# Two graph layers on one core: bit-packed adjacency stored per pair of groups, and catching up from tile 12 instead of 16

## What is computed

```python
def layer0(x, adj, weight, bias):
    a = adj.astype(x.dtype)
    x1 = a @ x / jnp.sum(a, axis=1, keepdims=True)
    return jnp.concatenate([x1, x], axis=1) @ weight + bias

def layer1(x, adj, W, a):
    h = jnp.einsum('ni,oi->no', x, W)
    e = (h @ a[:128])[:, None] + (h @ a[128:])[None, :]
    e = jnp.where(adj == 0, -jnp.inf, e)
    return jax.nn.softmax(e, axis=1) @ h

x = layernorm(x + layer0(x, adj, ...))
x = layernorm(x + layer1(x, adj, ...))
```

## Time and profile before

| | us |
|---|---|
| median of 3 runs | 1045.35 |
| lowest, highest | 1044.92, 1046.54 |
| the profiled execution, its own time | 1044.53 |
| its span, first to last instruction | 1042.8 |
| TensorE (PE) busy | 998.2 (96%) |
| VectorE (DVE) busy | 686.2 (66%) |
| ScalarE (ACT) busy | 607.9 (58%) |
| GpSimd (POOL) busy | 288.5 (28%) |

### The profile page before, as it was taken

How to read it: one execution, slowest core, us unless ns; L and a number is a source line. 1 busy time by engine, 2 the same in 40 slices (tenths; PEclk the granted TensorE clock), 3 DMA queues, 4 the chain that set the end, 5 groups by cost and what they waited for, 6 DMA issues and landing times.

```text
span 1042.8 us, 22097 instructions
## 1 busy us (share of the span) xinstructions
PE 998.2 (96%) x8783; PEld 872.1 (84%) x8783; DVE 686.2 (66%) x1647; ACT 607.9 (58%) x618; POOL 288.5 (28%) x275
## 2 busy tenths in 40 slices
PE   7898988999999999999999999999999999999996
PEld 6787867878888888888888888888888888888885
DVE  2677677787777767777676665555545765566564
ACT  2897798888888888888767676767421000000000
POOL 4344444443544445344332232222000000000000
PEclk8999999999999999999999999999999999999999
DMA  9999999999999999999999999999321112222101
GB/s 273 354 417 424 421 421 420 421 421 421 421 422 420 421 416 419 417 419 419 400 385 366 356 346 349 330 337 312 144 82 73 50 45 85 87 87 87 29 27 33
DMA packets 52569, 306.94 MB, mean 294 GB/s; under 512 B 6768, under 2 KB 8432, under 8 KB 19312
## 3 DMA queue, kind: packets, MB, share of 16 engines
q0 software_dynamic: 37344, 270.03, 65.5%
q1 hardware_dynamic: 14288, 34.71, 9.7%
q10 hardware_dynamic: 832, 0.75, 0.3%
HBM read 287.08 MB, written 18.38 MB: 293 GB/s over the span
## 4 chain that ended last, share of the span: by engine, by line
PE 63%; DMA 25%; ACT 6%; issue 3%; DVE 1%; POOL 1%; ACTq 0%; DVEq 0%
PE ps_agg L373 34%; DMA adj_in<-in_adj_dram,chunk 24%; PE ps_part L373 23%; ACT edges L562 5%; PE ps_y L373 4%; DMA x_all<-in_x_dram 1%; POOL adj_in L1335 1%; PE ps_h L745 1%; PE ps_h L683 1%; ACT parts L554 0%; PE ps_x1T L738 0%; ACT L578 0%; DVE partial L890 0%; DVE edgesT L921 0%; PE ps_y L683 0%
## 5 line engine op out<-in xcount | busy, mean ns | idle before, releaser
L373 PE MATMUL ps_agg<-parts,edgesT 128*128 128x257 f16 (+1 forms) x5248 | 606.2, 275 | 26.2 <-DVE edgesT L921 26.0
L373 PEld LDWEIGHTS ps_agg<-parts,edgesT 128*128 128x128 fp8e4 x5248 | 513.6, 98 | 106.0 <-DVE edgesT L921 30.5
L562 ACT ACTIVATE edges<-adj_in 128x2048 fp8e4<-128x2048 int32 x256 | 480.7, 1904 | 68.9 <-DMA adj_in<-in_adj_dram,chunk 68.6
L1335 POOL DMA_INDIRECT adj_in<-in_adj_dram,chunk x256 | 283.5, 1107 | 442.0 <-ACT edges L562 429.9
L921 DVE STREAM_TRANSPOSE edgesT<-edges 128x512 uint32<-128x512 uint32 x256 | 168.4, 691 | 71.5 <-ACT edges L562 70.7
L373 PE MATMUL ps_part<-parts,edgesT 128*128 128x258 f16 x1664 | 194.7, 273 | 0.0
L373 PEld LDWEIGHTS ps_part<-parts,edgesT 128*128 128x128 fp8e4 x1664 | 162.7, 98 | 22.8
L628 ACT ACTIVATE std<-mean_var,eps 128x1 f32<-128x1 f32 x64 | 18.9, 295 | 234.2 <-DVE mean_var L1158 234.2
L934 DVE SCALAR_TENSOR_TENSOR packed<-edgesT,packed 128x2048 uint32<-128x2048 uint32 x48 | 109.8, 2287 | 0.0
L373 PE MATMUL ps_part<-parts,packed 128*128 128x258 f16 x784 | 90.6, 273 | 0.0
L373 PEld LDWEIGHTS ps_part<-parts,packed 128*128 128x128 fp8e4 x784 | 76.6, 98 | 11.1
(11 more groups left out here) (118 smaller groups left out, 658.8 us busy)
## 6 DMA issues: line engine op xcount, KB each, us to landing
adj_in<-partial_sums SPq DMA_DIRECT2D x16, 258.0 KB, 5.8
adj_in<-in_adj_dram,chunk POOLq DMA_INDIRECT x256, 12.7
out_dram<-edges SPq DMA_DIRECT2D x60, 64.0 KB, 3.1
partial_sums<-partial SPq DMA_DIRECT2D x13, 258.0 KB, 7.2
packed_adj<-packed SPq DMA_DIRECT2D x3, 1024.0 KB, 9.5
adj_in<-packed_adj SPq DMA_DIRECT2D x2, 896.0 KB, 7.3
adj_in<-packed_adj SPq DMA_DIRECT2D x2, 832.0 KB, 4.9
x_all<-in_x_dram POOLq DMA_DIRECT2D x6, 256.0 KB, 10.0
```

The costliest lines, as they stand in the source:

```text
L373: done = eng.matmul(bank[:, 0:cols], rows[:, n // BYTES, n % BYTES, :], moving[:, n, :], start=(n == first), stop=(n == last))
L562: act.activation(edges[:, r // 2, r % 2, :], adj_in[:, m % SLOTS, :], ACT.Copy, scale=EDGE[t % GROUP], saturate=False).then_inc(s_conv, 1)
L1335: pool.indirect_dma_start(adj_in[:, m % SLOTS, :], None, adj_chunks, bass.IndirectOffsetOnAxis(chunk[:, 0:1], 0), element_offset=first_row ...
```

## The change

Two groups 2p and 2p + 1 (for the first 14 groups, `PAIRS` = 7) are joined into one word array: the odd group's words are shifted up by one bit and or-ed with the even group's (`join`), in place in `packed[:, 1]`, and stored once. The bits kept are now 4, 6, 2 and 0, so that the bit above each is free, and the edge values are 128, 128, 192 and 144. Groups 14 and 15 are stored alone. The second pass loads each group's words from its pair's store and takes the tile's bit out with one shift and mask. On VectorE the join of a pair stands in step 8p + 8 in the place of `pack`, whose two calls follow in step 8p + 9; the checks of the odd groups come in steps 8p + 7 and 8p + 8. On SyncE the partial sums are now stored ahead of the words. Catching up runs in tiles 12 to 23 with 2, 3 and 3 bands, in the bank `ps_small`, from two loads instead of three.

```diff
--- before.py
+++ after.py
@@ -48,8 +48,8 @@
     EARLY = FIRST_INLINE * GROUP
-    CATCH = 16
-    CAUGHT = [3, 3, 2]
+    CATCH = 12
+    CAUGHT = [2, 3, 3]
     CTILES = GROUP * len(CAUGHT)
     CWORDS = P * max(CAUGHT)
@@ -73,11 +73,14 @@
-    EDGE = [128.0, 128.0, 128.0, 192.0]
-    KEPT = [0x10, 0x20, 0x40, 0x04]
-    FOREIGN = 0x8B
-    UNPACKED = [2.0 ** -5, 2.0 ** -3, 2.0, 2.0 ** -6]
-    BIT_SCALE = [bit / edge for bit, edge in zip(UNPACKED, EDGE)]
+
+    EDGE = [128.0, 128.0, 192.0, 144.0]
+    KEPT_BIT = [4, 6, 2, 0]
+    KEPT = [1 << bit for bit in KEPT_BIT]
+    FOREIGN = 0x8A
+    UNPACKED_BIT, UNPACKED = 4, 2.0 ** -5
+    BIT_SCALE = [UNPACKED / edge for edge in EDGE]
+    PAIRS = GROUPS // 2 - 1
     def every_byte(b):
         return b * 0x01010101
@@ -99,7 +102,15 @@
     def last_turn(j):
         return turn_of[GROUP * loads[j] + GROUP - 1]
-    packed_dram = nc.dram_tensor("packed_adj", (GROUPS, P, TW), u32, kind="Internal").ap()
+
+    def store_of(g):
+        return g // 2 if g < 2 * PAIRS else g - PAIRS
+
+    def stored_bit(g, c):
+        return KEPT_BIT[c] + (g % 2 if g < 2 * PAIRS else 0)
+
+    STORES = store_of(GROUPS - 1) + 1
+    packed_dram = nc.dram_tensor("packed_adj", (STORES, P, TW), u32, kind="Internal").ap()
     part_dram = nc.dram_tensor("partial_sums", (GROUPS, P, GROUP * HCOLS), fp32, kind="Internal").ap()
     h_dram = nc.dram_tensor("g_h_rows", (N, HCOLS), fp32, kind="Internal").ap()
     x1_dram = nc.dram_tensor("g_x1_rows", (N, F), fp32, kind="Internal").ap()
@@ -181,9 +192,10 @@
         CBLOCK = 36
         late = parts1[:, CBLOCK:NBLK, :].rearrange("p n f -> p (n f)").bitcast(u32)
-        sizes = [len(CAUGHT) * CWORDS, 2 * CWORDS, len(CAUGHT) * GROUP * HCOLS, HCOLS]
+        c_loads = store_of(len(CAUGHT) - 1) + 1
+        sizes = [c_loads * CWORDS, 2 * CWORDS, len(CAUGHT) * GROUP * HCOLS, HCOLS]
         ends = list(itertools.accumulate(sizes))
-        c_in = late[:, 0:ends[0]].rearrange("p (k w) -> p k w", k=len(CAUGHT))
+        c_in = late[:, 0:ends[0]].rearrange("p (k w) -> p k w", k=c_loads)
         c_words = late[:, ends[0]:ends[1]].rearrange("p (k w) -> p k w", k=2)
         c_part = late[:, ends[1]:ends[2]].bitcast(fp32).rearrange("p (k c f) -> p k c f", k=len(CAUGHT), c=GROUP)
         c_lo = late[:, ends[2]:ends[3]].bitcast(fp32)
@@ -206,7 +218,7 @@
         ps_h = ps("ps_h")
         ps_small = ps("ps_small")
         sums = [ps_agg[0], ps_agg[1], ps_part, ps_y]
-        ps_caught = ps_catT
+        ps_caught = ps_small
@@ -239,6 +251,7 @@
         s_tr = sem("quarter_transposed")
         s_check = sem("checked")
         s_pack = sem("tile_packed")
+        s_joined = sem("pair_joined")
         s_pkst = sem("packed_stored")
         s_agg = sem("agg_summed")
@@ -287,7 +300,7 @@
         s_vord = sem("verdict_steps")
         s_flag = sem("flag_made")
-        s_cld = [sem(f"caught_words_landed{k}") for k in range(len(CAUGHT))]
+        s_cld = [sem(f"caught_words_landed{k}") for k in range(c_loads)]
         s_cunp = sem("caught_words_unpacked")
         s_csum = sem("caught_summed")
         s_clo = sem("caught_lo_copied")
@@ -424,11 +437,15 @@
             sp.dma_start(w1_sb[:, :], w1).then_inc(s_const1, 16)
             sp.dma_start(a2_sb[:, :], a1[F:2 * F].rearrange("(p o) -> p o", o=1)).then_inc(s_const1, 16)
-            def store_group(g):
-                words = slice(bands_of(g) * P, TW)
-                sp.wait_ge(s_pack, GROUP * (g + 1))
-                wait(sp, s_pkst, 16 * g)
-                sp.dma_start(packed_dram[g][:, words], packed[:, g % 2, words]).then_inc(s_pkst, 16)
+            def store_words(g):
+                n, words = store_of(g), slice(bands_of(g - 1 if g < 2 * PAIRS else g) * P, TW)
+                if g < 2 * PAIRS:
+                    sp.wait_ge(s_joined, n + 1)
+                else:
+                    sp.wait_ge(s_pack, GROUP * (g + 1))
+                    sp.wait_ge(s_check, CHECKS * g)
+                wait(sp, s_pkst, 16 * n)
+                sp.dma_start(packed_dram[n][:, words], packed[:, g % 2, words]).then_inc(s_pkst, 16)
             def store_partial(g):
                 sp.wait_ge(s_partk, GROUP * (g + 1) - EARLY)
@@ -437,35 +454,34 @@
             def load_caught(k):
                 sp.wait_ge(s_pkst, 16 * (k + 1))
-                sp.dma_start(c_in[:, k, 0:P * CAUGHT[k]], packed_dram[k][:, 0:P * CAUGHT[k]]).then_inc(s_cld[k], 16)
+                sp.dma_start(c_in[:, k, :], packed_dram[k][:, 0:CWORDS]).then_inc(s_cld[k], 16)
             def store_caught(k):
                 sp.wait_ge(s_ckept, GROUP * (k + 1))
                 sp.dma_start(part_dram[k], c_part[:, k, :, :].rearrange("p c f -> p (c f)")).then_inc(s_cst, 16)
             for g in range(GROUPS - 1):
-                store_group(g)
                 if g >= FIRST_INLINE:
                     store_partial(g)
-                if g == 2:
-                    load_caught(0)
-                    load_caught(1)
-                if g == 3:
-                    load_caught(2)
+                if g % 2 == 1 or g >= 2 * PAIRS:
+                    store_words(g)
+                if g % 2 == 1 and store_of(g) < c_loads:
+                    load_caught(store_of(g))
                 if 0 <= g - CATCH // GROUP < len(CAUGHT):
                     store_caught(g - CATCH // GROUP)
-            sp.wait_ge(s_pkst, 16 * (GROUPS - 1))
+            sp.wait_ge(s_pkst, 16 * (STORES - 1))
             sp.wait_ge(s_check, CHECKS * (GROUPS - 1))
             words0 = slice(done_of(0) * P, TW)
-            sp.dma_start(packed[:, 0, words0], packed_dram[0][:, words0]).then_inc(s_pkld[4], 16)
-            store_group(GROUPS - 1)
+            sp.dma_start(packed[:, 0, words0], packed_dram[store_of(0)][:, words0])\
+                .then_inc(s_pkld[4], 16)
+            store_words(GROUPS - 1)
             store_partial(GROUPS - 1)
             def load_group(j):
                 g, s = loads[j], (j - 1) % 4
                 words = slice(done_of(g) * P, TW)
-                sp.wait_ge(s_pkst, 16 * (g + 1))
-                sp.dma_start(packed_in[:, s, words], packed_dram[g][:, words]).then_inc(s_pkld[s], 16)
+                sp.wait_ge(s_pkst, 16 * (store_of(g) + 1))
+                sp.dma_start(packed_in[:, s, words], packed_dram[store_of(g)][:, words]).then_inc(s_pkld[s], 16)
                 if g >= FIRST_INLINE:
                     sp.wait_ge(s_partst, 16 * (g - FIRST_INLINE + 1))
                 sp.dma_start(part_in[:, s, :], part_dram[g]).then_inc(s_partld[s], 16)
@@ -754,7 +770,7 @@
             def caught(i):
                 blocks = GROUP * CAUGHT[i // GROUP]
                 if i == 0:
-                    pe.wait_ge(s_xTlc, GROUPS - AHEAD)
+                    pe.wait_ge(s_shift, 1)
                 pe.wait_ge(s_cunp, i + 1)
                 wait(pe, s_ckept, i)
                 contract(pe, ps_caught, c_words[:, i % 2, :], parts1, range(blocks), 0, blocks - 1).then_inc(s_csum, 1)
@@ -925,8 +941,10 @@
                 dve.wait_ge(s_tr, NQ * (t + 1))
                 bits, word = edgesT[:, t % 2, :], packed[:, g % 2, :]
                 if c == 0:
-                    wait(dve, s_pkst, 16 * (g - 1))
-                    wait(dve, s_check, CHECKS * (g - 1))
+                    if g % 2 == 0:
+                        wait(dve, s_joined, g // 2)
+                    else:
+                        wait(dve, s_pkst, 16 * (g // 2))
                     dve.tensor_single_scalar(word, bits, every_byte(KEPT[c] | FOREIGN), ALU.bitwise_and)\
                         .then_inc(s_pack, 1)
                 else:
@@ -941,6 +959,13 @@
                 dve.scalar_tensor_tensor(stray[:, :], packed[:, g % 2, part * width:(part + 1) * width],
                                          every_byte(FOREIGN), stray[:, :],
                                          ALU.bitwise_and, ALU.bitwise_or).then_inc(s_check, 1)
+
+            def join(p):
+                words = slice(bands_of(2 * p) * P, TW)
+                dve.wait_ge(s_pack, 2 * GROUP * (p + 1))
+                dve.wait_ge(s_check, 2 * CHECKS * (p + 1))
+                dve.scalar_tensor_tensor(packed[:, 1, words], packed[:, 1, words], 1, packed[:, 0, words],
+                                         ALU.logical_shift_left, ALU.bitwise_or).then_inc(s_joined, 1)
             def degree(t):
                 dve.wait_ge(s_agg, t + 1)
@@ -1028,6 +1053,8 @@
                 blk = slice(QBLK * s, QBLK * (s + 1))
                 dve.tensor_reduce(x_big[:, blk], parts0[:, blk, 0:F], AX.X, ALU.max, apply_absolute_value=True)\
                     .then_inc(s_xbig, 1)
+
+            odd_groups = range(1, 2 * PAIRS, 2)
             def step(t):
                 if on(t, 0) and t > 0:
@@ -1051,16 +1078,24 @@
                     moments_joined(t - 1)
                 if inline(t - 1):
                     keep_partial(t - 1)
-                if on(t, 0):
```

(33 more changed lines are left out.)

## The result

The changed kernel takes 1035.11 us in the median of 5 runs (1034.05 to 1036.87), beside 1044.92 us (1044.17 to 1046.54) for the kernel before on the same chip: a ratio of 0.9911, 95% interval 0.9899 to 0.9923, or 9.3 us less (8.0 to 10.6). Forecast was 1036.0, a gain of 9.0.

The account below looks back on a forecast made before the run. DMA's rate was taken to bound the kernel until tile 33, PE afterwards. Fewer bytes start tile 34 9.0 us earlier, other terms zero: 1044.53 - 9.0 = 1035.5, 1036.3 with the median's 0.8, given as 1036.0; range 1033.0 to 1041.5.

Parts of the forecast that it names:

- The bound: First pass: DMA engines' rate, about 421 GB/s, sets tile starts until tile 33; from tile 34 PE alone sets the end.
- The size: Before tile 33: 52 fewer bands stored (8.1 us), 0.3 us fewer reads; tile 34 starts 9.0 us earlier.
- The joins at nothing: DVE, step 8p + 8: seven joins, 11.0 us in all, covered by idle time or busy PE, cost zero.
- The catching up at nothing: Tiles 12 to 27: catching up from 12 leaves PE's sum the same and costs nothing at tile 33.
- Can PE follow: Tiles 5 to 33: PE has 20.5 us of gaps, 8.4 wanted; its ceiling is 10.2 us, about 1.2 above the gain.
- The port: Indirect DMA issues: joins may delay seven by 2.0 us each, covered by loads in flight; zero, far bound 14 us.
- the remaining gaps: PE in the first pass: gaps left would stand after the pairs' stores, at tiles 9 or 10, 17 or 18, 25 and 33.
- rival 2: Stores of packed words are hidden anyway, indirect loads being limited by their own queue: 1044.5 to 1045.4 us; chance 0.08.
- rival 1: ACT and DVE take PE's place, steps 8p + 7 and 8p + 8 half exposed: 4.6 us lost, 1040; chance 0.16.
- rival 3: DVE's step decides: joins and moved checks before tile 33, 12.9 us, all exposed; 3.9 us slower, 1048.4; chance 0.07.
- Rival 4: More than forecast: PE left only its own chain, a lower-clock tile (1.6 us) spared too; 1033 to 1034; chance 0.07.

Follow-up runs that it names:

- the second store: Changed kernel with each pair's words stored a second time, into a buffer nobody reads: 1043.96 us, ratio 0.9997 to the kernel before.
- the four pairs: Changed kernel with only groups 0 to 7 joined and groups 8 to 15 stored alone: 1034.43 us, ratio 0.9906 to the kernel before.
- the variant of before: Kernel before with only the catching up moved to tiles 12 to 23 (2, 3, 3 bands, other bank): 1044.06 us, ratio 1.0000.
- the narrow joins: Changed kernel with joins working on the last band only, 128 words instead of up to 2048: 1034.77 us, ratio 0.9909 to the kernel before.
- the heavier joins: Changed kernel with two more VectorE checks of 1.22 us ahead of every join: 1037.43 us, ratio 0.9932 to the kernel before.
- The combined kernel: Changed kernel, catching up from 16, pairs 0 and 1 stored in halves, pair 3's store after tile 34's pack, caught sums stored behind tile 39: 1032.54 us.
- pair 3 held back: Changed kernel with pair 3's store issued after the pack of tile 34 instead of in step 32: 1034.45 us, ratio 0.9904 to the kernel before.
- the halves: Changed kernel with each pair's store cut in two, the second half issued after the pack of tile 8p + 10: 1035.34 us, ratio 0.9915.

## Why the prediction was right

**The bound.** DMA's rate up to tile 34 and PE's work after it: shown by the second store, which took back 8.9 us, and by the four pairs, which took back nothing. Where stores were moved or doubled, the data of tile 34 followed the count of bytes to within 0.3 us each time (8.90 us later for 8.7 counted; 0.65, 1.51, 1.95 and 3.53 earlier for 0.8, 1.7, 1.7 and 3.6), also where PE hid it.

**The size.** 9.0 us at tile 34 against 9.13 and 9.20 measured. The step was a count of bands at 0.156 us; the second store measures 8.91 / 56 = 0.159 us for one. That the total is so close has some luck in it. The sum was 8.4 us for DMA, and 0.7 because DMA needs 9.96 us from tile 33 to 34 where PE needed 10.64. Measured, the data of tile 34 came 8.1 us earlier (359.82 to 351.70), and the rest, 1.0 us, is PE's lag behind them before (1.07 us) less that now (0.06). Both terms are off by 0.3 us, in opposite directions. Tile 33 itself came 9.45 us earlier and not 8.4: the forecast held some of pair 3's store to lie ahead of it, but its last transpose came 9.7 us earlier, and holding that store back moved tile 33 no more than tile 32 (0.3 us each).

The Trainium skill (DMA: Bandwidth & Descriptors, section Bandwidth) gives 341 GB/s for a load of 1 MB measured by itself; by an estimate from that figure the 56 bands of the second store would be 10.8 us. The traces do not agree: 8.9 us, beside a stream of loads at 421 GB/s in all.

**The joins at nothing.** Right, and shown by taking them nearly out. One of 2048 words took 2292 ns (2287 forecast), all seven 11.4 us. "The later three joins lie under a busy PE" gave the wrong reason, though: what covers them is 1.2 us ahead of one instruction, the low parts, and what is added beyond that in their step shows, under a busy PE too.

**The catching up at nothing.** Right in both kernels, within the 1.0 us by which the one profile of the variant of before is off.

**Can PE follow.** Right in the sum, with less room than the step said. It put PE's ceiling 1.2 us above the gain. It left out that a pair's store, half as often and later, makes one longer gap (4.12 us at tile 10, 3.0 at tile 26), behind which the tile may run at the lower clock for 1.6 us more. With that, and with what PE loses elsewhere, PE's room at tile 34 was 0.2 us in one execution and 0.3 in the other, not 1.2. The forecast placed the remaining gaps at 9 or 10, 17 or 18, 25 and 33; they came at 10, 18, 26 and, with 0.17 us, 34 in the one execution. It did not name those before tiles 6, 7 and 8 (0.93, 0.91 and 1.01 us), which stayed as they were.

**The port.** POOL's indirect DMAs took 1076 ns in the mean instead of 1107, in spite of seven joins; and taking the joins out changed nothing. That the loads in flight cover such delays fits this and is not shown by a run of its own.

**Rivals.** The stores are not hidden (rival 2 fell by the second store); ACT and DVE did not take PE's place (rival 1 fell by the narrow joins, and since the last conversion before tile 34 waits for DMA; the moved checks were not taken out in any run); rival 3 would have needed an exposure of 9 us, and 17 us of added work in the heavier joins cost 3.5 by tile 49. Rival 4, more than forecast, did not come by the change itself: the two jobs gave 9.3 and 9.9 us, and rival 4 wanted 10.5 at least. The combined kernel brought 2.2 us more at tile 34.

## What to carry to other kernels

Where a stream of loads is the bound and another engine takes over later, price every other transfer in bytes, but only those ahead of the tile where the bound changes hands; here 54 bands counted and the rest did not. When two bounds end within a microsecond of each other, moving one lets only part of its worth through (0.6 of 2.0 us with pair 3 held back) or shows a loss where the move makes a new gap (the halves). Then follow each bound by itself, here by the end of the last transpose beside the start on PE: it shows whether the step that was moved did its part. An operation that seems free on an engine at 67% is free by the distance to the one consumer behind it: look for the wait that would come next, and add a known amount there to measure it.

## What the runs showed that I had not expected

Whether TensorE's clock falls to its lower level behind a gap is not a matter of the gap's length alone. Over all profiles, tiles 5 to 63: behind gaps of 1.9 to 3.1 us it went both ways. A tile of 8.97 us instead of 7.33 came for instance behind 1.94, 2.09, 2.80, 3.00 and 3.12 us, and tiles at the upper clock behind 2.01, 2.51, 2.97, 3.02 and 3.12 us; the same tile 26 of the same kernel went both ways in two executions. Behind gaps up to 1.89 us no tile ran at the lower clock, and behind the nine of 3.77 us and more all did. So a chain of PE's work that holds a gap of 2 to 3 us can differ by 1.6 us from one execution to the next. What decides it the traces do not show.
